# Order of scatters and result writes on GpSimd in the expert stage of a two-layer transformer kernel

## The reference

```
x1 = layernorm(x + attn_out, g1, be1)
gate_probs = softmax(x1 @ Wg + bg)              # 8 experts
topk_p, topk_i = top_k(gate_probs, 2); topk_p /= sum(topk_p)
comb = sum(one_hot(topk_i, 8) * topk_p[..., None], axis=-2)
h = gelu(einsum('bsd,edf->bsef', x1, W1) + b1)  # 512 hidden
y = einsum('bsef,efd->bsed', h, W2) + b2
x = x + layernorm(x1 + einsum('bse,bsed->bsd', comb, y), g2, be2)
```

## Time and profile before

| | |
|---|---|
| median of 3 runs | 1571.78 us (1570.97 to 1571.88) |
| profiled execution, its own time | 1570.05 us |
| span of its trace | 1568.3 us |
| mean granted TensorE clock | 0.947 |
| PE busy | 1387.2 us, 88% |
| DVE busy | 1236.8 us, 79% |
| ACT busy | 1142.7 us, 73% |
| POOL busy | 513.9 us, 33% |

### The profile page before, as it was taken

How to read it: one execution, slowest core, us unless ns; L and a number is a source line. 1 busy time by engine, 2 the same in 40 slices (tenths; PEclk the granted TensorE clock), 3 DMA queues, 4 the chain that set the end, 5 groups by cost and what they waited for, 6 DMA issues and landing times.

```text
span 1568.3 us, 36364 instructions
## 1 busy us (share of the span) xinstructions
PE 1387.2 (88%) x13425; PEld 605.9 (39%) x13425; DVE 1236.8 (79%) x2031; ACT 1142.7 (73%) x2357; POOL 513.9 (33%) x821
## 2 busy tenths in 40 slices
PE   5769999999999899679999999999989999899970
PEld 2323433333333466212222222222222235788960
DVE  6788888888885266899999999999999963453375
ACT  7618888888888666239999998899878997333441
POOL 5412334333333477300000002100221334556663
PEclk9959999999999999859999999999999999899995
DMA  4622111111212354301333331112101413667864
GB/s 139 196 93 75 47 65 58 56 65 58 67 48 91 98 162 140 127 24 49 122 130 127 109 99 37 44 51 77 53 35 43 130 36 94 191 184 230 271 197 127
DMA packets 127089, 158.62 MB, mean 101 GB/s; under 512 B 17280, under 2 KB 99712, under 8 KB 126656
## 3 DMA queue, kind: packets, MB, share of 16 engines
q1 hardware_dynamic: 116800, 129.21, 26.5%
q0 software_dynamic: 10112, 27.08, 4.7%
HBM read 90.99 MB, written 69.21 MB: 102 GB/s over the span
## 4 chain that ended last, share of the span: by engine, by line
PE 43%; DVE 11%; issue 4%; DMA 4%; ACT 3%; POOL 1%; SPq 1%; POOLq 0%; ACTq 0%; DVEq 0%
PE bank L642 16%; PE banks L627 9%; DVE row_max L681 6%; PE banks L583 6%; PE banks L1568 3%; PE banks L1578 3%; PE banks L1461 2%; ACT o_sums L742 1%; DMA expert_results<-k_work,row_of 1%; POOL expert_results L1369 1%; DMA sorted_in<-v_all,slots 1%; DMA parts<-sorted_in 1%; PE banks L350 1%; DMA probs<-expert_results 1%; DVE probs L375 1%
## 5 line engine op out<-in xcount | busy, mean ns | idle before, releaser
L681 DVE TENSOR_REDUCE row_max<-banks 128x2 f32<-128x1024 f32 (+3 forms) x896 | 933.9, 1103 | 61.5 <-PE banks L583 33.1
L727 ACT ACTIVATE probs<-banks 128x512 f32<-128x512 f32 (+3 forms) x1792 | 875.2, 552 | 115.1 <-PE banks L627 93.1
L642 PE MATMUL bank<-probs,v_ones 128*32 128x256 f32 (+2 forms) x6656 | 521.3, 385 | 12.0 <-ACT o_sums L742 10.8
L583 PE MATMUL banks<-k_work,q_work 48*128 48x512 bf16 (+3 forms) x1792 | 357.7, 375 | 55.3 <-DVE row_max L681 46.6
L627 PE MATMUL banks<-q_work,k_work 51*128 51x512 bf16 (+3 forms) x1792 | 376.5, 367 | 11.1 <-ACT probs L727 9.9
L627 PEld LDWEIGHTS banks<-q_work,k_work 51*128 51x128 bf16 x1792 | 104.7, 93 | 378.7 <-ACT probs L727 341.9
L642 PEld LDWEIGHTS bank<-probs,v_ones 128*32 128x32 f32 x6656 | 133.7, 108 | 257.3 <-ACT probs L727 172.9
L768 POOL DMA_DIRECT2D heads_out<-o_sums x64 | 36.7, 574 | 469.4 <-ACT o_sums L742 469.4
L2160 ACT ACTIVATE rope<-banks,expert 128x256 f32<-128x256 f32 x184 | 72.2, 475 | 119.0 <-PE banks L1568 119.0
L788 POOL TENSOR_SCALAR_AFFINE_SELECT probs<-probs 128x256 f32<-128x256 f32 x256 | 103.9, 409 | 125.0 <-ACT probs L727 124.3
L583 PEld LDWEIGHTS banks<-k_work,q_work 48*128 48x128 bf16 x1792 | 90.2, 95 | 111.8 <-DVE row_max L681 87.0
(11 more groups left out here) (207 smaller groups left out, 1080.0 us busy)
## 6 DMA issues: line engine op xcount, KB each, us to landing
expert<-expert_rows SPq DMA_DIRECT2D x46, 578.0 KB, 4.5
qk_parts<-parts SPq DMA_DIRECT2D x64, 256.0 KB, 2.7
heads_out<-o_sums POOLq DMA_DIRECT2D x64, 256.0 KB, 3.7
sorted_in<-front SPq DMA_DIRECT2D x21, 520.0 KB, 6.3
q_work<-qk_parts SPq DMA_DIRECT2D x64, 128.0 KB
k_work<-qk_parts SPq DMA_DIRECT2D x64, 128.0 KB
parts<-sorted_in SPq DMA_DIRECT2D x46, 130.0 KB, 4.0
q_work<-qk_parts SPq DMA_DIRECT2D x64, 64.0 KB
```

The lines of the kernel that those rows point to most:

```text
L583: last = pe.matmul(to[:, par, 0:width], q[r:r + M0, pair, qt * P:(qt + 1) * P], k[r:r + M0, pair, kh * G:kh * G + width], start=True, stop ...
L642: last = pe.matmul(bank[7][32 * j:32 * j + 32, c0 + c1:c0 + c1 + w], v_ones[i % QB][:, kt, j, :], prob_slots[:, (e + j) % RING, c1:c1 + w] ...
L681: dve.tensor_reduce(row_max[:, :, pair, qt, kh], self.buf_of("chunk", g, c)[:, :, 0:width], AX.X, ALU.max).then_inc(self.s["chunk_max"], 1)
L727: act.activation(prob_slots[:, e % RING, 0:width], self.ring_bank("exp", e)[:, 0:width], ACT.Exp, scale=SCALE).then_inc(s["exps"], 1)
```

## The change

One line of constants. `GIVEN_FIRST` says which blocks' results stand before the second part of batch 3's scatters and which before `shares(1)`; `GIVEN_TILES` says after which of batch 4's tiles one block's results are put in between. Before, blocks 0 to 2 stand after the first 12 scatters of section 1, blocks 3 to 5 after the next four, and blocks 6, 7 and 8 after two, four and six tiles of batch 4. Now no results stand before the last scatter; the loops over `GIVEN_FIRST` are empty, and all 46 blocks follow in order.

```diff
-        GIVEN_FIRST, GIVEN_TILES = (3, 6), (2, 4, 6)
+        GIVEN_FIRST, GIVEN_TILES = (0, 0), ()
```

## The result

| | median of 15 runs | lowest to highest |
|---|---|---|
| before | 1573.71 us | 1570.47 to 1578.83 |
| changed | 1579.39 us | 1574.23 to 1583.23 |

The ratio is 1.0031 with a 95% interval of 1.0021 to 1.0042: about 4.9 us slower (3.3 to 6.6). The changed kernel's median is 2.8 us above the forecast 1576.6; 1.9 of that is before's own median, which is 1573.71 in these 15 runs and was 1571.78 in the three that the forecast started from. The profiled execution took 1577.39 us, with a span of 1575.6 us and a mean granted clock of 0.944.

The account below looks back on a forecast made before the run. POOL's chain to its last result DMA was taken to bound the end: -8.8 (scatters) + 24.0 (nine blocks) - 10.4 (idle time) = +4.8 us, a median of 1576.6 us, own range 1574 to 1580, with rivals 1569.4 to 1581.1.

Parts of the forecast that it names:

- The free slots: POOL before batch 4's scatters: taking 12 result DMAs out gains 0; the first scatter stays at 1378.75.
- The scatters of batch 4: POOL, 16 scatters: seven periods of 4.40 us per pair, first result at 1412.1, 8.8 us earlier.
- Nine blocks more behind them: POOL after the last scatter: 18 more result DMAs at 1.331 us each, 24.0 us more.
- Blocks 9 to 32: POOL's result writes up to the first root: 63.9 us as before, their data having been there long.
- rival C: Result writes: loss comes from later DMAs landing more slowly; moving roots alone gives 0.999 to 1.001; no chance given.
- The idle time: POOL ahead of the first tail_root: all 10.38 us of waiting for DVE's moments goes; root at 1500.0.
- The boundary: PE at section 1's start: its 2.4 us wait for rows goes, moments at 1492.5, worth nothing at the end.
- the first rival: Batch 4's scatters at 2.7 us a pair, then moments decide: 2.4 us faster, 1569.4 us; chance 0.11.
- The tighter waits: SP's load_y(0) and DVE's keep_y wait for later results: load_y(0) has some 4 us left.
- The sum: At POOL's last result and the end: -8.8 + 24.0 - 10.4 = +4.8 us.
- theory D: On some chips, POOL's back-to-back indirect DMAs keep other queues and engines unserved, causing the 30 to 45 us standstill.
- rival E: After the last scatter: PE stands still 30 us or more, from chip and program place, whatever POOL does; no chance given.

Follow-up runs that it names:

- e2: Before with only blocks 6, 7 and 8 moved behind the last scatter, blocks 0 to 5 in their old places; ratio to before 1.0011.
- f4: Repeat of e2 in another set: before with only blocks 6, 7 and 8 moved behind the last scatter; ratio to before 0.9995.
- e6: The changed kernel with up to four of batch 4's scatters in flight instead of two; ratio to before 0.9974.
- f2: The changed kernel run again without an edit, in a set with the standstill; ratio to before 1.0069.
- e4: The changed kernel with the four tail_root steps moved behind blocks 13, 16, 19 and 21; ratio to before 1.0037.

## Why the prediction was right, and where a step was off

**The free slots.** Right. `shares` waited 7.04 us for the gap and the first scatter 2.04 us for the slots: taking twelve DMAs out there gained nothing. The other side, that there is no loss with these six blocks in place, was measured in e2 and f4, on chips on which POOL idles for over 21 us ahead of the root; there it holds, but the sum doesn't describe these chips. The first scatter of batch 4 moved off 1378.75, which was named as a sign of being wrong; 2.5 of the 2.9 us are older than anything that was moved.

**The scatters of batch 4.** Right in sum, though not in kind. From the first scatter to the first result 33.35 us were forecast and 32.73 measured. The single periods run from 2.7 us (1385.44 to 1388.17) to 5.4 us (1388.17 to 1393.62), wider than the 3.8 to 5.0 of the earlier trace rows; their mean, (1413.07 - 1382.94) / 7 = 4.30, is close to the 4.40 I took.

**Nine blocks more behind them.** Forecast 24.0 us, measured 1438.20 - 1414.34 = 23.9.

**Blocks 9 to 32.** Forecast 63.9 as before, measured 1504.52 - 1438.20 = 66.3. This term was mis-sized by 2.4 us: a result DMA took 1.38 us instead of 1.331, at a DMA share of 0.91 instead of 0.83. The loads of picked results for DVE (from 1486.93) now fall in this stretch, where before they came just behind it; that they are the cause is argued and not tested. For it: the first 20 of these DMAs still go at 1.327 us each, and the last seven periods before the end, from 1492.59 to 1503.54, at 1.56. This is what is true of rival C, that result DMAs get slower when they come later: 2.4 us of the loss. That their data had been there long, the prediction's reason for the old pace, was not the whole condition. The last 13 blocks and their roots took 1544.82 - 1504.52 = 40.3 instead of 42.5, and give 2.2 of it back.

**The idle time.** Right: 10.38 us became 0, and the root went from +116.3 to +122.9 (forecast +121.3). The measured terms are -9.4 (scatters), +23.9 (nine blocks), +2.5 (blocks 9 to 32), -10.4 (idle time) and -2.2 (the rest): the idle time and the shorter row of scatters are why 24 us of added work cost only 4.4. e6 shows the limit from the other side: brought forward by more than that, POOL waits for the moments again.

**The boundary.** Wrong in its words, without effect on the sum: PE's 2.4 us wait for section 1's rows was to go, and 2.1 us of it stayed. I had put it down to the landing of the scatters alone. In before that landing does end last (1419.60 + 3.13 = 1422.73), but right behind it stands SP's own order: with the landing out of the way, SP came to the load at +43.0 instead of +44.8, and no earlier, and the load took 4.76 us instead of 3.31. The moments are therefore 0.4 us earlier and not 2.4, and the first rival, whose gain rested on this, would have been worth some 0.4 us.

**The tighter waits.** Right: `load_y(0)` went out at +105.3 instead of +105.7, so no later than in before. The 4.96 us used there as the landing of a scatter is a period of the earlier trace rows, which a landing can't exceed but may fall short of; nothing in the sum hung on it.

**The sum.** Forecast +4.8, measured +4.4 in the two traces and +4.9 in the ratio. That it agrees so closely is in part luck: +2.4 in blocks 9 to 32 is offset by -0.6 in the scatters and -2.2 in the last 13 blocks, and the two traces are one execution of each kernel, while executions of one kernel spread over 8 to 9 us. Of the signs named, the first result at 1414.34, the root at 1504.52 and the last result at 1544.82 lie 0.3, 2.5 and 0.8 us above their ranges as clock times, and inside them less the 2.9 us by which everything starts later.

**What stays open.** In the sets with the standstill the change costs 1.0069, more than the sum explains. The root is at +142.7 to +145.6 in the five traces with blocks 0 to 5 in their free slots and at +158.7 to +161.7 in the three without; but those without start batch 4's scatters at 1386 to 1391 us and the others at 1392 to 1401, so part of the standstill only moves. That the row of DMAs causes it (theory D) has two things for it: the traffic of exactly that row, and that the standstill ends in all eight traces just after POOL has to wait. It was argued from traces only. The one run that takes the row away did not meet such a chip, so rival E is not excluded.

## What to carry to other kernels

When an engine that ends last has an idle stretch earlier on, work that is added ahead of that idle time costs only what doesn't fit into it; so look for the last idle time on the queue of the engine that ends the chain, and count up to there and from there. Such an idle time is also the first thing to remove: here four short steps that wait stood ahead of results that were ready, and the fastest kernel of the study (0.9948) has them moved by a few places, together with three blocks' results. The move by itself was measured only where there is a standstill (0.9977 and 0.9962). And when a landing that holds a load is brought forward, the issuing engine's own order may come right behind it; see when it gets to the load.

## What the runs showed of the hardware

One indirect DMA of 128 rows costs POOL 0.96 us and the next starts 1.26 us after it at the earliest. With up to four in flight they go at nearly that pace (e6: 16 scatters and the step to the first result in 22.0 us, 1.38 us each), with two in flight beside the loads of weights the mean is 4.3 us a pair.

I had not expected that the same program behaves in two ways in one stretch, in sets that ran on different chips; whether the chip or something else about a set decides it isn't known. On two of the chips, while POOL issued result DMAs in a row, there was a stretch in which no other queue had a packet (f2, 1450 to 1468) and PE, ACT, DVE and SP stood still, PE for up to 31.6 us at once (e4). Within it (f2, 1441.47) eight products take 3.75 us that take 1.89 otherwise, at a granted clock of 0.50, the 1.2 GHz level. In the traces of before and of the changed kernel the same row of DMAs runs nearly as fast (1.33 and 1.38 us each) while the core moves 247 and 277 GB/s, and PE is busy 61.67 of 64.07 us and 65.70 of 66.30.
